# Expert blocks behind a two-expert router: who fills the pads, when the block counts are read, and where the bias constants are computed

## What is computed

```python
x = x + attention_a(layernorm(x))        # 16 heads of 64, causal softmax
x = x + ffn(layernorm(x))                # experts, first time
x = x + attention_b(layernorm(x))        # linear attention, 8 heads of 128, and a gated MLP
x = x + ffn(layernorm(x))                # experts, second time

# ffn, with E = 8 experts of width F = 512 and K = 2 chosen for each token
probs = softmax(xn @ Wr + br)
scores, idx = top_k(probs, K)
full = relu(xn @ W1_e + b1_e) @ W2_e + b2_e          # for each expert e
c = einsum('ef,efh->eh', relu(b1), W2) + b2
c_total = c.sum(axis=0)
output = sum_k scores_k * (full[idx_k] - c[idx_k] + c_total)
```

## Time and profile before

| | us |
|---|---|
| median of 3 runs | 1403.65 |
| lowest, highest | 1402.89, 1404.59 |
| the profiled execution | 1405.29 |
| its span, first to last instruction | 1403.4 |
| TensorE busy in it | 1228.9 (88%) |
| VectorE, ScalarE, GpSimd busy | 928.5, 822.5, 515.8 |

### The profile page before, as it was taken

One profiled execution on the slowest core, in us unless ns is written; L12 is line 12 of the kernel. 1 busy time (PEld: TensorE's weight loads), 2 busy tenths in 40 slices (PEclk: granted clock), 3 DMA queues, 4 the chain that ended last, 5 costly groups with the idle time before them and its releaser, 6 DMA issues. The chain is left out here.

```text
span 1403.4 us, 27110 instructions
## 1 busy us (share of the span) xinstructions
PE 1228.9 (88%) x7787; PEld 929.0 (66%) x7787; DVE 928.5 (66%) x3602; ACT 822.5 (59%) x2478; POOL 515.8 (37%) x683
## 2 busy tenths in 40 slices
PE   6999999999999996699967999999997877089990
PEld 5666666666666764499955777777774644079990
DVE  6778888888887885244446888888773655244445
ACT  5888888888888884044423555555654654044440
POOL 2112333332423233255432344434332455535541
PEclk9999999999999998799987999999998999589996
DMA  9100000000000000222220000000000011222226
GB/s 291 35 1 1 9 9 9 9 13 7 13 8 13 7 11 16 58 70 70 71 82 24 16 16 15 16 1 0 2 1 1 26 33 33 64 57 70 69 71 190
DMA packets 54445, 52.92 MB, mean 38 GB/s; under 512 B 7341, under 2 KB 43098, under 8 KB 54330
## 3 DMA queue, kind: packets, MB, share of 16 engines
q1 hardware_dynamic: 39584, 30.98, 7.8%
q0 software_dynamic: 8928, 17.84, 3.8%
q10 hardware_dynamic: 5818, 2.73, 0.7%
HBM read 29.48 MB, written 22.05 MB: 37 GB/s over the span
## 5 line engine op out<-in xcount | busy, mean ns | idle before, releaser
L1337 ACT ACTIVATE prob<-prob,negmax 128x512 f32<-128x512 f32 (+3 forms) x512 | 283.0, 556 | 78.4 <-DVE negmax L1434 76.5
L1434 DVE CUSTOM_DVE_ANT_0 prob<-bank,mask 128x512 f32<-128x512 f32 (+3 forms) x512 | 227.8, 483 | 50.6 <-PE bank L1150 50.1
L1509 POOL TENSOR_TENSOR Vs<-Vh_sb,rinv 128x256 f32<-128x256 f32 x128 | 78.2, 611 | 364.5 <-DVE rinv L1411 364.3
L1038 POOL DMA_INDIRECT expert_out<-f_x_yb,f_x_to x142 | 136.1, 958 | 172.5 <-DVE f_x_yb L1024 111.0
L1167 PE MATMUL bank<-prob,Vs 128*64 128x512 f32 (+3 forms) x1024 | 151.9, 439 | 0.9 <-DVE zT_lo L1406 0.9
L675 POOL DMA_INDIRECT expert_in<-f_xn,f_slot x128 | 126.6, 989 | 47.5 <-issue 29.2
L961 PE MATMUL bank<-f_x_xbT,W_sb 128*128 128x256 f32 x568 | 138.4, 388 | 1.6 <-DVE f_x_xbT L1004 1.5
L985 ACT ACTIVATE f_x_hid<-bank,cols 128x256 f32<-128x256 f32 x144 | 63.0, 474 | 98.8 <-PE bank L961 98.8
L961 PEld LDWEIGHTS bank<-f_x_xbT,W_sb 128*128 128x128 f32 x568 | 104.6, 194 | 14.6 <-DVE f_x_xbT L1004 2.8
L985 ACT ACTIVATE prob<-bank,cols 128x256 f32<-128x256 f32 x140 | 61.3, 473 | 86.8 <-PE bank L961 86.8
L1167 PEld LDWEIGHTS bank<-prob,Vs 128*64 128x64 f32 x1024 | 63.4, 136 | 69.4 <-issue 59.5
(11 more groups left out here) (263 smaller groups left out, 3199.6 us busy)
## 6 DMA issues: line engine op xcount, KB each, us to landing
f_x_xb<-expert_in SPq DMA_DIRECT2D x73, 130.0 KB
b_crows<-expert_out SPq DMA_DIRECT2D x16, 256.0 KB, 2.7
c_crows<-expert_out SPq DMA_DIRECT2D x16, 256.0 KB, 4.0
expert_out<-f_x_yb,f_x_to POOLq DMA_INDIRECT x142
x_sb<-in_L_attn_a_x_dram SPq DMA_DIRECT2D x8, 256.0 KB, 6.9
W_sb<-in_L_ffn_W_dram SPq DMA_DIRECT2D x1, 2048.0 KB, 9.8
expert_in<-f_xn,f_slot POOLq DMA_INDIRECT x128
out_dram<-x_sb ACTq DMA_DIRECT2D x8, 256.0 KB, 3.8
```

The source lines that it names most:

```text
L1038: pool.indirect_dma_start(yg, bass.IndirectOffsetOnAxis(ap=self.to[:, t:t + 1], axis=0), self.yb[:, t, :], None).then_inc(self.stored[t], 16)
L1337: nc.scalar.activation(mine, mine, ACT.Exp, scale=-1.0, bias=negmax[:, n % 4, t, a:a + 1], accum_out=rowsum[:, n % 4, t, a:a + 1]).then_in ...
L1434: nc.vector.tensor_tensor_reduce(out=prob[:, n % 4, a, columns_of(n, which)], in0=bankS[which][a][:, 0:width[i]], in1=mask[:, T - width[i] ...
L1509: nc.gpsimd.tensor_tensor(Vs[:, m % 4, :, :].rearrange("p t (a d) -> p t a d", a=2), V_sb[:, quarter % 2, small:big + 1:big - small, pair] ...
```

## The change

Four things are done.

- Each expert's pads have a semaphore of their own. ScalarE writes those of experts 0 to 3, SyncE those of experts 4 to 7. SyncE waits for an expert's pads ahead of that expert's loop, and for all scatters ahead of the first.
- The block counts are read by `load_counts`, called apart from `each_block` and handed to it. TensorE and VectorE call it behind the plan and ahead of the rest of the folding; SyncE calls it ahead of its fills, GpSimd ahead of its two priming DMAs; ScalarE behind its fills (and in the first expert stage behind the value-output evacuations).
- The counters of the expert stage are brought to START at the beginning of the whole stage, with those of the route.
- The 64 bias matmuls of L740 are done in two halves: experts 0 to 3 behind `pe_first`, ahead of the last row's transposes; experts 4 to 7 behind the last row's rank, ahead of `pe_count`. The sum over experts is the first step of `pe_third`. VectorE computes the constant and its diagonal form ahead of WVO_lo. ScalarE's evacuation of the value-output products is split off as `act_third`, behind its fills.

```diff
+            def pe_c(self, pe, some):
                 pe.wait_ge(self.rb1_ready, E)
                 pe.wait_ge(s_big, 96)
-                for e in range(E):
+                for e in some:
                     for c in range(FC):
                         mm = nc.tensor.matmul(self.bankC[0:E, 0:D], self.rb1[:, e, c, :], W2_sb[:, e, c, :],
                                               start=(e == 0 and c == 0), stop=(e == E - 1 and c == FC - 1))
-                mm.then_inc(self.c_done, 1)
+                if E - 1 in some:
+                    mm.then_inc(self.c_done, 1)
+
+            def pe_third(self, pe):
+                pe.wait_ge(self.c_ready, 1)
+                pe.wait_ge(self.b2_c_ready, 1)
+                nc.tensor.matmul(self.bankC[0:E, 0:D], ones[:, 0:E], self.c[:, :], start=True,
+                                 stop=True).then_inc(self.csum_done, 1)
                 pe.wait_ge(self.scaled, 1)
...
-                self.filled = [sem(f"{name}_x_filled_{of}", at) for of in ("sp", "act")]
+                self.filled = [sem(f"{name}_x_filled{e}", at) for e in range(E)]
...
+                self.of_pe = (self.transposed, *self.up_done, *self.down_done)
+                self.of_act = (*self.hid_ready,)
+                self.of_dve = (self.xbT_ready, self.meta_ready, self.this_to_ready, self.second_known,
+                               *self.to_ready, *self.y_ready)
+
+            def load_counts(self, eng):
+                eng.wait_ge(self.plan_ready, 2)
+                return [eng.value_load(blocks[0:1, e:e + 1], min_val=1, max_val=MAX_BLOCKS) for e in range(E)]
...
-                n = [eng.value_load(blocks[0:1, e:e + 1], min_val=1, max_val=MAX_BLOCKS) for e in range(E)]
                 if before is not None:
                     before()
                 for e in range(E):
+                    if between is not None:
+                        between(e)
                     with eng.Fori(0, n[e]) as i:
...
-            BY_SP = 6
+            BY_ACT = 4
...
                 def rows_written():
-                    sp.wait_ge(self.filled[0], 16 * self.BY_SP)
-                    sp.wait_ge(self.filled[1], 16 * (E - self.BY_SP))
+                    self.fill(sp, range(self.BY_ACT, E))
                     for u in range(route.ring):
                         sp.wait_ge(route.scattered[u], PRIMED + len(range(u, B, route.ring)) * 16 * TOP * NT)
+                def pads_written(e):
+                    sp.wait_ge(self.filled[e], 16)
...
                     folding.pe_first(pe)
+                    folding.pe_c(pe, range(0, E // 2))
                     route.norm.pe_transpose(pe, B - 1, 1)
                     route.pe_logits(pe, B - 1, 1)
                     folding.pe_second(pe)
                     route.pe_rank(pe, B - 1, 1)
                     pe.wait_ge(zT_ready, START + B * PAIRS)
                     pe.wait_ge(x_done, START + B)
+                    folding.pe_c(pe, range(E // 2, E))
                     experts.pe_count(pe, route)
+                    counts = experts.load_counts(pe)
                     folding.pe_third(pe)
-                    experts.pe_work(pe)
+                    experts.pe_work(pe, counts)
...
                     folding.act_second(act)
-                    experts.fill(act, range(experts.BY_SP, E), experts.filled[1])
-                    experts.act_work(act)
+                    experts.fill(act, range(experts.BY_ACT))
+                    folding.act_third(act)
+                    experts.act_work(act, experts.load_counts(act))
...
                     experts.dve_plan(dve, route)
+                    counts = experts.load_counts(dve)
                     folding.dve_c(dve)
                     folding.dve_last(dve)
...
-                    experts.fill(sp, range(experts.BY_SP), experts.filled[0])
-                    experts.sp_work(sp, route)
+                    experts.sp_work(sp, experts.load_counts(sp), route)
```

More of the change, by code:

```diff
@@ L814, in dve_last @@
                                             A_hi[:, four, :], ALU.subtract).then_inc(self.low, 1)
[L815 to L821, removed]
                 dve.wait_ge(self.csum_done, 1)
@@ L829, in dve_last @@
                                         ALU.mult).then_inc(self.diag_ready, 1)
+                for k in range(2):
+                    four = slice(4 * k, 4 * k + 4)
+                    dve.wait_ge(self.VO_hi_ready, k + 1)
+                    nc.vector.scalar_tensor_tensor(
+                        out=WVO_lo[:, four, DB:], in0=self.bankVO[k][:, :].rearrange("p (h e) -> p h e", e=D),
+                        scalar=DB ** 0.5, in1=WVO_hi[:, four, DB:], op0=ALU.mult,
+                        op1=ALU.subtract).then_inc(self.low, 1)
                 for g in range(2):
@@ L874, in __init__, with each_block @@
                 self.name = name
-            def each_block(self, eng, body, before=None):
+                self.of_pe = (self.transposed, *self.up_done, *self.down_done)
[5 more added lines that the diff above has]
+                return [eng.value_load(blocks[0:1, e:e + 1], min_val=1, max_val=MAX_BLOCKS) for e in range(E)]
+            def each_block(self, eng, n, body, before=None, between=None):
                 count = eng.alloc_register(self.name + "_block")
@@ L917, in dve_plan, with fill @@
                                         ALU.max).then_inc(self.plan_ready, 1)
[L919 to L921 removed]
+            BY_ACT = 4
+            def fill(self, eng, some):
                 eng.wait_ge(self.plan_ready, 2)
@@ L938, in rows_written, with pe_work @@
                 def rows_written():
-                    sp.wait_ge(self.filled[0], 16 * self.BY_SP)
-                    sp.wait_ge(self.filled[1], 16 * (E - self.BY_SP))
+                    self.fill(sp, range(self.BY_ACT, E))
                     for u in range(route.ring):
                         sp.wait_ge(route.scattered[u], PRIMED + len(range(u, B, route.ring)) * 16 * TOP * NT)
-                end, _ = self.each_block(sp, lambda e, row, k, k16: load(row, k), rows_written)
+                def pads_written(e):
+                    sp.wait_ge(self.filled[e], 16)
+                end, _ = self.each_block(sp, n, lambda e, row, k, k16: load(row, k), rows_written, pads_written)
                 load(0, end)
-            def pe_work(self, pe):
-                begin(pe, self.transposed, *self.up_done, *self.down_done)
-                pe.wait_ge(self.plan_ready, 2)
+            def pe_work(self, pe, n):
                 def transpose(k, k16):
@@ L973, in expert, with act_work @@
                         mm.then_inc(self.down_done[t], 1)
[L975 to L979, removed]
+                self.each_block(pe, n, expert, lambda: transpose(START, START))
+            def act_work(self, act, n):
                 def relu(e, row, k, k16):
@@ L987, in relu, with dve_work @@
                                              ).then_inc(self.hid_ready[c], 1)
[L989 to L994, removed]
+                self.each_block(act, n, relu)
+            def dve_work(self, dve, n):
                 def prepare(k, k16):
@@ L1039, in store @@
                                                 self.yb[:, t, :], None).then_inc(self.stored[t], 16)
-                _, end16 = self.each_block(pool, store)
+                _, end16 = self.each_block(pool, n, store)
                 for t in range(BT):
@@ L1115, in _ @@
                 def _(pe):
-                    begin(pe, q_done, k_done, v_done, scores_done, z_done, outT_done, row_done, ahead.tr, *route.of_pe)
+                    begin(pe, q_done, k_done, v_done, scores_done, z_done, outT_done, row_done, ahead.tr, *route.of_pe, *experts.of_pe)
                     def project_Q(b, u, g):
@@ L1494, in _ @@
                     dve.wait_ge(folding.moe_copied, 2)
-                    experts.dve_work(dve)
+                    experts.dve_work(dve, counts)
                 @block.gpsimd
@@ L2015, in _ @@
                     def _(pe):
-                        begin(pe, turned, gate_done, up_done, row_done, *route.of_pe)
+                        begin(pe, turned, gate_done, up_done, row_done, *route.of_pe, *experts.of_pe)
                         def turn(b):
```

38 lines of the change are left out of this document (16 added, 22 removed).

## The result

The changed kernel takes **1394.28 us** (median of six runs, 1392.88 to 1396.84) against 1403.08 (six runs, 1401.96 to 1404.59). The ratio is 0.9941, 95% interval 0.9930 to 0.9952: faster by 8.8 us, where 14.5 were forecast. The profiled execution took 1395.62 us around a span of 1393.3.

A forecast was written before the change was run, and what follows sets the result against it. At two hand-overs from the last row's routing to the expert blocks, engines wait for one serial chain. A -11.7, B -3.5, added costs +0.7 make -14.5 us: 1403.65 to 1389.2 us, range 1383 to 1397.

The forecast's parts named there:

- Hand-over A, the folding: Routing to expert blocks near 560 us, plan's end to first evacuation: folding frees VectorE at 576.8, gaining 11.7 us.
- SyncE must keep up: At hand-over A: SyncE's counts, four fills and load land at 575.6, 1 us ahead of the folding.
- Hand-over B: Routing to expert blocks near 1212 us, plan's end to first evacuation: SyncE's queue alone bounds it; gains 3.5 us.
- The plan at A: End of the last row's routing before hand-over A: 1.0 us earlier, at 560.5, bounds 559 and 565.5.
- the unnamed wait of the earlier trace: Before the plan at A: `place` at 559.01 had waited 3.55 us for something the trace can't name.
- Added costs: Early counter releases: +0.5 us at the MLP stage's start, +0.2 at the kernel's start, sum +0.7.
- the two lots of L740: Sign at A: bias matmuls come in two lots of 32, the first ending before the last row's transposes.
- the second: Rival, 0.11: fills and scatters in flight slow SyncE's counts; B gains nothing, or at A +3.7, 1396.4 us.
- The first: Rival, 0.12: clock not kept at A, second half of bias matmuls holds the count back; +5.0, 1394.2 us.
- The third: Rival, 0.10: everything keeps full clock and SyncE's queue is last at A and B; 1382.4 us.
- the fourth: Rival, 0.06: A isn't shortened, as counts ahead of the folding and slow loads, clock and products push it; 1397.9 us.
- the fifth: Rival, 0.03: each expert block's pass takes longer, paid some 71 times; at 0.3 us a block, 1410.5 us.

The follow-up runs named there:

- fills_first: Changed kernel, but SyncE again issues six fills ahead of its counts and ScalarE the other two behind its evacuations; 1398.69 us, ratio 0.9959.
- fold_as_before: Changed kernel, but the folding, with TensorE's and VectorE's counts, is in its old order; new fills and early releases kept; 1404.36 us, ratio 1.0008.
- in_pairs: Changed kernel, but GpSimd waits after every second scatter of the last row until those have landed; 1396.72 us, one run.
- fills_late: Changed kernel, but ScalarE's four fills wait until all scatters have landed; 1397.36 us, ratio 0.9948.

## Why the prediction was right, and where it was not

The direction, the two places and the range held; the gain was 5.7 us smaller than forecast, because one term, SyncE's counts, was costed at half its price at A and at 60% of it at B. By its own steps:

- **Hand-over A, the folding: right, and its time partly by luck.** VectorE was to be free at 576.8 and was at 577.15, with the counts to 567.9 (567.0 forecast) and the clock at 0.50 through the products. But the plan came 1.5 us late. From the plan's end the folding took 15.1 us instead of 16.3: counts 5.9 for 6.5, products 3.8 for 3.4, and above all the broadcast 2.3 (granted clock 0.84) for 3.3. The reordering shortens A (fills_first). That the releases take the load out from behind the folding shows in fold_as_before, where it goes at 576.72 with VectorE in the folding until 583.31; in the changed kernel it went behind the folding's end all the same.
- **"SyncE must keep up": this step failed.** Its counts were costed at 4.5 to 5 us and took 10.3. The fills were costed at 1.93 each and took 1.16 (573.08 to 576.57 for three intervals), which gave 3.1 back. The load went at 577.89 instead of 573.4, behind the folding's last operation and not ahead of it, and landed at 580.5, so A ended at 581.37, not 576.8: **4.6 us**, of which 1.5 is the plan's lateness (below) and 3.1 this queue. Of these, 0.84 us is a term that the sum left out: when the load is last, TensorE's transposes of the first block stand between its landing and the evacuation (580.53 to 581.37), so that SyncE's lead in the forecast was 0.4 us and not 1. in_pairs shows the counts at 5.3 in the same place when the scatters come in pairs.
- **Hand-over B: the same term.** Counts at 9.2 instead of 5.5, fills at 1.16 instead of 1.95: the distance shrank by 1.9 instead of 3.5, **1.6 us** short. The step from the earlier trace rows to "fills and scatters out together" was the error: these rows show ScalarE's counts at 9.4 us while both were out, and I charged half of it to the fills. The rows could not tell the two apart; that GpSimd's scatters were out until 1220.63 in the earlier trace rows, and the steps ended 1.6 us later, was there to be read.
- **The plan at A: wrong by 1.5 us.** It was to come 1.0 us earlier and came 0.5 later, with 0.3 of that already at the last row's statistics (542.72, before 542.40). The clock was kept as hoped (1.00 where the earlier trace rows have 0.51) and the rank came 2.9 us earlier (554.07, before 556.93). It bought nothing, since the place stood until 1.6 us behind the end of the second-last row's burst. I had kept part of the gain back for the unnamed wait of the earlier trace rows; all of it should have been.
- **Added costs: the size right, one of the two places wrong.** The MLP stage's first transpose comes 0.3 us later behind the start of its normalisation, 0.5 were forecast. At the kernel's start nothing shows of the 0.2 forecast: up to 435 us the rows' statistics come no later than before (435.35, before 435.49). But from there to the last row's statistics the changed kernel takes 107.4 us and the kernel before 106.9, and all nine variants take 107.3 to 107.5. Part of it is a wait of VectorE for TensorE (1.07 us instead of 0.72, at 503.5). I had not forecast it, and its cause is open. The blocks kept their pace at A (581.37 to 715.68, 134.3 us; 134.5 before) and were 0.9 us shorter at B.

Counting in the traces: plan +0.5, A -7.7, from there to B -0.2, B -1.9, the blocks of B -0.8: -10.1, which is the spans' difference, 4.4 short of the forecast. A and B miss 6.2; the blocks of B give 0.8 back and the stretches of the added costs 0.9 (-0.2 measured from A to B, +0.7 forecast). The medians differ by 8.8, another 1.3 less, as single executions do.

Of the signs that the prediction set, the two lots of L740, the clock above 0.51 and TensorE's counts straight behind the plan came; the plan by 561.5 (562.01), the load before L836, L1004 by 580 (581.37), and at B the load within 15 us (15.25) and L1004 within 18 (18.69) did not. None of those that would have made it wrong came.

Of the rivals, the second named the right bottleneck and nearly its price (L1004 near 580.5, 1396.4 in all) under a wrong condition, fills and scatters; fills_late took the fills away and the stretch stayed. Its part at B, no gain, didn't come either: 1.9. The first has the measured time to 0.1 us (1394.2) by chance, for the clock was granted at 0.98 to 1.00 up to the count, and the second half of the bias matmuls, until 560.2, held it by less than the slot did (TensorE waited 0.18 us more for that). The third fell with the same counts and with the clock of 0.50 in the products, the fourth with the 7.2 us that L1004 came earlier, the fifth with the blocks. The rule that the prediction cites from the Trainium skill, "DMA: Bandwidth & Descriptors", section "Issuing engines are not separate DMA queues", is that spreading transfers over issuing engines saves only the time to issue them. The runs agree: the load goes 2.2 us earlier behind the plan than in fills_first, which is the issue of two fills. The one sign of transfers in each other's way is the load of fills_late at B, 1.1 us longer beside ScalarE's fills.

## What to carry to other kernels

When a change leaves two queues within a microsecond of each other, the forecast hangs on the cheaper-looking one: cost its small instructions from rows of the very stretch in which they will stand, not from a quiet one. Take work off the queue that leads to the first load and issue it where a later loop has room; here that was worth nearly as much again as the whole change (0.9883 against 0.9941). A wait whose releaser the trace can't name is not a reserve: find what ends at the same moment in every trace that you have.

## What the runs showed of the hardware

- Some 4 us into an unbroken run of GpSimd's indirect scatters (0.96 us each, one every 1.26), register instructions and waits of other engines begin to come in steps of 0.70 to 0.73 us, until 1.4 to 1.7 us behind the last. In the changed kernel SyncE's steps begin at 565.4 and 1207.1, in runs that begin at 561.09 and 1203.44. They show on SyncE most, on ScalarE and GpSimd, and before the change on VectorE at B (690 ns in the earlier trace rows). VectorE and TensorE can go on longer: both read their eight counts at A until 568 with no instruction over 0.61 us, and in the burst that begins at 547.76 TensorE's matmuls run 0.11 us apart until 556.6 and then 0.7 apart until 559.2. Pairs with a pause of 1.8 to 2.4 us between them show none on SyncE (one execution), and behind the six unbroken scatters ahead of B's route, whose last ended at 1200.4, the place started within 0.2 us of the rank's end, so length alone is not the whole condition. What lies behind it was not tried.
- TensorE's granted clock was 0.62 of full, as a mean of the next 9 us, behind a gap with 1.18 us of work in 3.4, and stayed at 1.00 behind the same gap filled with small matmuls.
- Executions of one kernel fall apart in the first 23 us: the second row's first statistics came at 21.9 to 22.4 us in some of the profiles and at 23.0 to 23.5 in the others, over kernels that don't differ there, and the 1.2 us are still there at the last row's statistics (541.5 to 541.9 against 542.7 to 543.1). I found no cause.
